# Sparse attention beside a mixture of experts: the weights of experts 10 to 15 loaded and split later, in halves, over the first 16 tiles

## The reference

```python
xn = _layernorm(x, axis=-1)
x = x + attn(xn, ...) + ffn(xn, ...)

# attn: 16 query heads, 4 key heads, two 32-wide parts (one with rope);
# keys and values of the first 896 tokens are averaged in 14 blocks of 64,
# the last 128 stay single
scores = (q_sem @ k_sem2 + q_geo @ k_geo2) * scale * exp(logit_scale)
probs = softmax(where(k_pos <= pos, scores, -1e9))
out = (probs @ v2) @ Wo

# ffn: 16 experts, the best 4 of each token
scores = softmax(x @ router_w.T + expert_bias)
top_w, top_idx = top_k(scores, 4); top_w = top_w / sum(top_w)
act = silu(x @ gate_proj[e]) * (x @ up_proj[e])      # 256 -> 224
out = sum over the 4 experts of top_w * (act @ down_proj[e])
```

## Time and profile before

| | us |
|---|---|
| median of 3 runs (lowest, highest) | 395.76 (393.83, 397.96) |
| profiled execution | 395.17 |
| its span | 393.4 |
| TensorE busy | 350.6 (89%) |
| VectorE busy | 242.4 (62%) |
| GpSimd busy | 232.0 (59%) |
| ScalarE busy | 182.6 (46%) |

### The profile page before, as it was taken

How to read it: one execution, slowest core, us unless ns; L and a number is a source line. 1 busy time by engine, 2 the same in 40 slices (tenths; PEclk the granted TensorE clock), 3 DMA queues, 4 the chain that set the end, 5 groups by cost and what they waited for, 6 DMA issues and landing times.

```text
span 393.4 us, 8217 instructions
## 1 busy us (share of the span) xinstructions
PE 350.6 (89%) x2085; PEld 287.6 (73%) x2086; DVE 242.4 (62%) x784; ACT 182.6 (46%) x530; POOL 232.0 (59%) x207
## 2 busy tenths in 40 slices
PE   0498997998979999987977999999999999999991
PEld 0393675645746677666876999999999999999881
DVE  3879996488458789852547455555555555555550
ACT  1540186458013344444455455555555555555550
POOL 0600456546664464659987466666666666666664
PEclk9998998699989999996998899999999999999996
DMA  7993112224146388863686476666776766666544
GB/s 247 361 314 89 55 60 84 75 80 125 69 147 209 114 257 257 248 213 86 174 176 100 71 113 107 112 107 107 110 113 108 111 112 112 109 108 107 70 52 53
DMA packets 50094, 52.33 MB, mean 133 GB/s; under 512 B 5632, under 2 KB 47120, under 8 KB 50072
## 3 DMA queue, kind: packets, MB, share of 16 engines
q0 software_dynamic: 14640, 19.34, 29.8%
q1 hardware_dynamic: 35432, 32.73, 29.1%
HBM read 30.14 MB, written 21.91 MB: 132 GB/s over the span
## 4 chain that ended last, share of the span: by engine, by line
PE 48%; DMA 18%; POOL 14%; issue 9%; DVE 6%; ACT 2%; POOLq 1%; SPq 1%; DVEq 0%; ACTq 0%
PE bank L1366 39%; DMA xn_by_expert<-x_all,slot_i 14%; POOL xn_by_expert L714 13%; PE bank L1728 4%; PE bank L1704 4%; DMA out_rows<-y,idx 2%; DMA x_all<-in_L_attn_x 1%; ACT x_all L763 1%; POOL wgu_lo L691 1%; DVE stats L954 1%; PE bank L1378 1%; DVE logit_left L1024 1%; DMA xg<-xn_by_expert 1%; POOLq L103 0%; ACT wgu_hi L815 0%
## 5 line engine op out<-in xcount | busy, mean ns | idle before, releaser
L741 POOL DMA_INDIRECT out_rows<-y,idx x79 | 124.5, 1576 | 66.3 <-ACT y L930 39.6
L714 POOL DMA_INDIRECT xn_by_expert<-x_all,slot_i x64 | 66.2, 1034 | 55.6 <-DMA xn_by_expert<-x_all,slot_i 33.7
L1366 PE MATMUL bank<-wgu_hi,xh 128*128 x158 | 65.9, 417 | 4.7 <-DVE wdn_lo L1195 2.6
L1346 DVE SCALAR_TENSOR_TENSOR act<-bank,xg,sg 128x224 f32<-128x224 f32 x79 | 35.6, 451 | 55.7 <-ACT sg L917 55.7
L1366 PE MATMUL bank<-wgu_lo,xh 128*128 x158 | 59.3, 375 | 0.0
L1366 PE MATMUL bank<-wgu_hi,xl 128*128 x158 | 58.8, 372 | 0.0
L917 ACT ACTIVATE sg<-bank 128x224 f32<-128x224 f32 x79 | 28.3, 358 | 62.3 <-PE bank L1366 62.3
L1338 DVE TENSOR_TENSOR xl<-bank,xh 128x256 fp32r<-128x256 f32 x79 | 33.5, 425 | 35.5 <-ACT xh L908 35.5
L1366 PE MATMUL bank<-wdn_hi,ah 112*128 x158 | 51.8, 328 | 0.6 <-issue 0.5
L1366 PE MATMUL bank<-wdn_hi,al 112*128 x158 | 44.8, 283 | 0.0
L1366 PE MATMUL bank<-wdn_lo,ah 112*128 x158 | 44.6, 282 | 0.0
(11 more groups left out here) (235 smaller groups left out, 658.2 us busy)
## 6 DMA issues: line engine op xcount, KB each, us to landing
xg<-xn_by_expert SPq DMA_DIRECT2D x79, 129.0 KB, 2.5
wgu<-in_L_ffn_gate_proj SPq DMA_DIRECT2D x16, 224.0 KB, 4.0
wgu<-in_L_ffn_up_proj SPq DMA_DIRECT2D x16, 224.0 KB, 4.6
wdn<-in_L_ffn_down_proj SPq DMA_DIRECT2D x16, 224.0 KB, 4.9
x_all<-in_L_attn_x SPq DMA_DIRECT2D x8, 256.0 KB, 5.0
xr<-in_L_attn_x SPq DMA_DIRECT2D x14, 128.0 KB, 2.2
out_rows<-xr SPq DMA_DIRECT2D x14, 128.0 KB, 3.8
out_rows<-y,idx POOLq DMA_INDIRECT x79, 3.8
```

Of the source, the lines that this page charges most:

```text
L714: gp.indirect_dma_start(xs_d, bass.IndirectOffsetOnAxis(slot_i[:, z, r:r + 1], 0), x_all[:, z, :], None).then_inc(xs_in[p], DMA)
L741: gp.indirect_dma_start(out_rows, bass.IndirectOffsetOnAxis(idx[r % RING][:, 0:1], 0), ysb[r % 4][:, :], None, compute_op=ALU.add).then_in ...
L1346: nc.vector.scalar_tensor_tensor(av[t.par][:, :], bank[2 + t.par][:, I:2 * I], xg[t.slot][:, D + 1:D + 2], sg[t.par][:, :], ALU.mult, ALU. ...
L1366: return nc.tensor.matmul(o, lhsT, rhs, start=start, stop=stop)
```

## The change

The experts' groups become (4, 5), (6, 7), (8, 9), (10, 11), (12, 13), (14, 15). SyncE loads (6, 7) after `store_sum(1)` and (8, 9) after `store_sum(3)`; (10, 11) behind tiles 0 to 3; (12, 13) and (14, 15) behind tiles 4 to 7. ScalarE splits (6, 7) in pair 3 as before, (8, 9) in pair 5, and the experts 10 to 15 in the steps 2 to 13 of the tile stage, one of the two copies per step. VectorE makes their low parts in the steps 4 to 15, one of the two differences per step. GpSimd's loop makes the low parts of 6 to 9 only. The written-out steps reach to 16 instead of 8, and TensorE waits for the tile's own expert up to tile 17. The planner gives every expert at least one task, so that the expert of task n is never above n.

```diff
-LATE = ((4, 5), (6, 7), (8, 9), (10, 11), (12,), (13,), (14, 15))
+LATE = ((4, 5), (6, 7), (8, 9), (10, 11), (12, 13), (14, 15))
...
-        SPLITS = ((), (4, 5), (), (6, 7), (8, 9), (10,), ())
-        HEAD = (11, 12)
+        SPLITS = ((), (4, 5), (), (6, 7), (), (8, 9), ())
         SENT = 11
         BETWEEN = (4, 5)
-        IN_LOOP = 13
+        IN_LOOP = 10
+        HIGH_FROM, LOW_FROM = 2, 4
...
         ROUND = 8
+        HEAD = 2 * ROUND
...
-            for r in range(-2, ROUND + 1):
+            for r in range(-2, HEAD + 1):
                 step(Tile(0, r))
             if carry:
-                carry()
-            with eng.Fori(1, rounds) as i:
+                carry(HEAD)
+            with eng.Fori(HEAD // ROUND, rounds) as i:
...
             load_residual(REMOTE - 1)
-            def load_behind(n, t):
-
-                for u in range(NB):
-                    sp.wait_ge(c_s[u], t)
-                load_late(n)
 
             for i in range(REMOTE - 3):
                 store_sum(i)
                 load_residual(i + 2)
-                if i < 3:
-                    load_late(i + 1)
-                else:
-                    load_behind(4, 2)
+                if i % 2:
+                    load_late(i // 2 + 1)
             store_sum(REMOTE - 3)
-            load_behind(5, 4)
...
             for j in range(RING // 2):
                 load_task(j, j)
+            load_late(3)
             for i in range(REMOTE - 2, REMOTE):
                 store_sum(i)
             for j in range(RING // 2, RING):
                 load_task(j, j)
-            load_late(6)
+            load_late(4)
+            load_late(5)
...
+            def split_high_part(e, part):
+                if part == 0:
+                    nc.scalar.copy(of_expert(wgu_h, e), of_expert(wgu, e))
+                else:
+                    nc.scalar.copy(of_expert(wdn_h, e), of_expert(wdn, e)).then_inc(w_hi, 1)
+
             def split_high(e):
-                nc.scalar.copy(of_expert(wgu_h, e), of_expert(wgu, e))
-                nc.scalar.copy(of_expert(wdn_h, e), of_expert(wdn, e)).then_inc(w_hi, 1)
+                for part in range(2):
+                    split_high_part(e, part)
...
-            def split_late(k):
-                if k == SENT:
...
-                split_high(k)
+            def split_late(k, parts=(0, 1)):
+                if 0 in parts:
+                    if k == SENT:
...
+                for part in parts:
+                    split_high_part(k, part)
...
                     for u in range(NB):
                         p_keep(u, Pair(0, REMOTE - 1))
-                    for k in HEAD:
-                        split_late(k)
...
-                if j.counts is None and j.r in (5, 6, 7):
-                    split_late(IN_LOOP + j.r - 5)
+                n = j.r - HIGH_FROM
+                if j.counts is None and 0 <= n < 2 * (E - IN_LOOP):
+                    split_late(IN_LOOP + n // 2, (n % 2,))
...
                 link(nc.vector.tensor_tensor(tasks[:, :], tiles_f[:, :], bound[:, 1, :], ALU.subtract))
+                link(nc.vector.tensor_scalar(tasks[:, :], tasks[:, :], 1.0, None, ALU.max))
...
-                if j.counts is None and j.r in (6, 7, 8):
-                    k = IN_LOOP + j.r - 6
-                    dve.wait_ge(w_lo, k)
-                    split_low(k)
+                n = j.r - LOW_FROM
+                if j.counts is None and 0 <= n < 2 * (E - IN_LOOP):
+                    k = IN_LOOP + n // 2
+                    if n % 2 == 0:
+                        dve.wait_ge(w_lo, k)
+                    split_low_part(k, n % 2)
...
-                    if t.counts is None and t.r <= ROUND + 1:
+                    if t.counts is None and t.r <= HEAD + 1:
                         pe.wait_ge(w_lo, pe.to_reg(e + 1))
```

More of the change, by code:

```diff
@@ L546, in steps @@
                 if carry:
-                    carry()
+                    carry(ROUND)
             for r in range(ROUND * rounds + 1, NS + 1):
@@ L873, in p_keep @@
                 last.then_inc(c_pT[u], 1)
-            def split_late(k):
-                if k == SENT:
[L877 to L881, removed]
-                split_high(k)
+            def split_late(k, parts=(0, 1)):
+                if 0 in parts:
+                    if k == SENT:
+                        for p in range(GT):
+                            act.wait_ge(xs_in[p], K * GROUPS * DMA)
+                    for n, ks in enumerate(LATE):
+                        if k == ks[0]:
+                            act.wait_ge(w_late[n], len(ks) * 3 * DMA)
+                for part in parts:
+                    split_high_part(k, part)
             def attention_act(t):
@@ L1190, in l_values, with split_low_part @@
                 nc.vector.tensor_copy(oT[u][:, 2 * g:2 * g + 2, :], bank[7][:, 0:2 * P].rearrange("p (j n) -> p j n", j=2)).then_inc(l_osb, 1)
+            def split_low_part(e, part):
+                if part == 0:
+                    dve.wait_ge(w_hi, e + 1)
+                    nc.vector.tensor_tensor(of_expert(wgu_l, e), of_expert(wgu, e), of_expert(wgu_h, e).bitcast(F32), ALU.subtract)
+                else:
+                    nc.vector.tensor_tensor(of_expert(wdn_l, e), of_expert(wdn, e), of_expert(wdn_h, e).bitcast(F32), ALU.subtract).then_inc(w_lo, 1)
             def split_low(e):
-                dve.wait_ge(w_hi, e + 1)
-                nc.vector.tensor_tensor(of_expert(wgu_l, e), of_expert(wgu, e), of_expert(wgu_h, e).bitcast(F32), ALU.subtract)
-                nc.vector.tensor_tensor(of_expert(wdn_l, e), of_expert(wdn, e), of_expert(wdn_h, e).bitcast(F32), ALU.subtract).then_inc(w_lo, 1)
+                for part in range(2):
+                    split_low_part(e, part)
             def keep_tables():
@@ L1679, in load_experts, with carry @@
                     known[first + k] = values[k]
-            def carry():
+            def carry(first):
                 for r in range(2):
-                    pe.reg_mov(carried[r], known[ROUND + r])
+                    pe.reg_mov(carried[r], known[first + r])
                 known.clear()
```

## The result

| | before | changed |
|---|---|---|
| median | 396.31 (4 runs) | 409.52 (4 runs, 409.29 to 410.07) |
| profiled execution | 395.17 | 409.47 |
| its span | 393.4 | 407.4 |

The changed kernel is slower: its time is 1.0408 of the one before, with an interval of 1.0356 to 1.046. The direction was forecast, the size was not: 9.1 us were forecast and 14.3 us came between the two profiled executions. On the median shown before, 395.76 us, the ratio stands for 411.9 us, above the upper end of the range (397.5 to 410).

The account below looks back on a forecast made before the run. The tile stage was taken to keep TensorE's pace, with only its start, gated by the dispatch, and run-up movable. 16.7 - 1.0 - 8.1 + 1.5 = +9.1 us on 395.17 made 404.3, given as 404.5 us; range 397.5 to 410.

Parts of the forecast that it names:

- Which views and which gate: Start of the tiles: the last scores, at 192.2, replace the dispatch, at 175.46, as the gate of tile 0.
- The loads in the attention: Pairs 3 and 5: late expert loads hold the splits and attends, with cold restarts; tile 0 16.7 us later (11.3 to 16.7).
- The entry: Ahead of tile 0: TensorE's idle shrinks from 3.19 to some 0.7 us and it may keep its clock; 1.0 us gained.
- The run-up: Early tiles: two TensorE gaps and their restarts go, 8.1 us gained; tile 8's load late behind weights, 1.5 us lost.
- the tile stage losing again what it gained: Sign of being wrong: the tile stage gives back its gain, pointing at tile 8's load or the scatters.
- the half splits: Twelve half splits on ScalarE (steps 2 to 13) and VectorE (4 to 15): costed at nothing, 0 to 2 us in all.
- the planner's instruction: Planner: one extra instruction on a 128x16 tile, 100 us ahead of any need; costed at nothing.
- the lighter dispatch: Dispatch: (10, 11), 12 and 13 no longer load beside it, but it is no gate any more; costed at nothing.
- The scatters beside VectorE's low parts: GpSimd's scatters in the tile stage: slowed by VectorE's differences beside them; taken as 0, bound 2.6 us.
- The hidden waits: Rival, faster: both groups land within ScalarE's cover, (6, 7) by 146.00, leaving only the gains; 386.3 us, chance 7%.
- The tile stage suffers too: Rival, slower: tile 8 late by 3 us and cold (+3.2), scatters held by VectorE (+2.6); 410.3 us, chance 15%.

Follow-up runs that it names:

- both repairs: Changed kernel with (6, 7) and (8, 9) loaded one turn earlier and tiles 8 to 11 loaded ahead of the last four experts: 384.19 us, ratio 0.9714.
- one group late in the kernel before: Kernel before with (6, 7) alone loaded one turn later, after the sum of pair 1, right ahead of (8, 9): 396.73 us, ratio 1.0029.
- tiles 4 and 5 first: Against the kernel with both repairs: tiles 4 and 5 loaded right behind tiles 0 to 3, ahead of (10, 11) and the last sums: 384.28 us.
- tiles first: Changed kernel with tiles 8 and 9 loaded ahead of (12, 13) and tiles 10 and 11 ahead of (14, 15): 401.92 us.
- empty issues: Changed kernel with (12, 13) and six 8 KB DMAs into scratch ahead of tile 8's load, (14, 15) after tile 11: 407.48 us.
- 8 idle products: Changed kernel with 8 products that nobody reads added in TensorE's gap before attend(4): 408.21 us.

## Why the prediction was right in its direction and wrong in its size

**Which views and which gate: right.** The loads of (6, 7) and (8, 9) hold ScalarE, ScalarE holds the attend, and the last scores replace the dispatch as the gate of tile 0. The experiments with the loads moved back show it for both groups together and for the second alone.

**The loads in the attention: 16.7 us forecast, 16.3 measured, and by luck, out of two wrong parts.** From VectorE's sum to the free split it took 151.15 - 139.50 = 11.7 and 176.29 - 165.03 = 11.3 us, not 13.17: the prediction took the place of (8, 9) as it stood, with (6, 7) in flight ahead of it. The time is saved before the loads, not in them: from the sum to the first issue it is 143.06 - 139.50 = 3.6 us instead of 146.33 - 141.03 = 5.3, from there to the free split 8.1 us instead of 7.9. The gaps were 6.3 and 5.8 us, where 8.2 and 7.7 had been forecast (the second with the 0.38 us of before). The first restart cost 158.33 - 152.82 = 5.5 instead of 151.37 - 147.83 = 3.5 us, 2.0 us and near the 1.7. The second cost 13.36 - 7.29 = 6.1 us: here the price from one row was far off. Gaps forecast 3.7 us too long and restarts 4.7 us too cheap nearly cancelled; and the changed kernel's execution came to pair 1's sum 1.5 us sooner. SyncE's store of the sum before is 1.5 us sooner too (130.13 against 131.66), ahead of the first load that the change moves, so I put this down to spread between executions.

**The entry: right.** 1.0 us forecast, 1.5 us measured. TensorE idled 1.01 us instead of 3.19 before tile 0 and stayed at the upper level (the last attend of the attention took 1.90 instead of 2.94 us). The gain reaches the tiles over SyncE: the last sums are stored sooner, and tile 4's load, which stands behind them, goes out 10.1 us behind tile 0's instead of 11.4.

**The run-up: here the prediction failed.** Its two gaps went as forecast (8.1 us by the rows, 8.6 us by the tiles' turns). The failed step is "late by as much as the 2.7 MB ahead of it take beyond their issue. I allow 0 to 3 us of wait and 0 to 1.7 us for a cold restart, and take 1.5 us lost". That term measured 7.8 us, with a wait of 6.0 us and the restart. The mechanism was named; its size was guessed and not worked out. The issue time in it was nearly right (11.0 us behind tile 4's load forecast, 11.8 measured). What was missing is the time of the bytes. With the 270 to 289 GB/s of the windows above, 2.75 MB take about 10 us; the twelve issues take 6.9 us (206.67 to 213.55). That alone would be some 3 us of wait. The rest fits the other traffic on the same engines: from the first of these issues to tile 8's landing (206.67 to 222.10) the window shows 262 GB/s, 4.0 MB, 1.3 MB more than the twelve loads; tiles 4 to 7 and the scatters were under way. Half the bytes with as many issues cut the wait to 0.79 us, and the other order removed it, with 5.8 us gained between tiles 4 and 14. With 7.8 for 1.5 the sum of the prediction is 15.4 us, against 14.3 us. The prediction's own sign of being wrong, "the tile stage losing again what it gained, which would point at tile 8's load", is what came.

**Costed at nothing, and rightly:** the half splits (from the turn of tile 9 to that of tile 14 the changed kernel keeps the pace of 2.38 us, 237.81 - 225.91 = 11.9 us; whole splits cost some 2.5 us), the planner's instruction, and the lighter dispatch, which was no gate. With both repairs it is the gate of tile 0 again, and there it counts.

**The scatters beside VectorE's low parts:** 0 was taken, and 0 it is. The 15 scatters from 207.44 to 248.72 took at most 1.62 us. In this order of work the difference ends as the scatter begins:

```profile
214.07 1.08 DVE L1198 TENSOR_TENSOR wgu_lo<-wgu,wgu_hi 128x896 fp32r<-128x896 f32 x1
```

It runs to 215.15, and the scatter beside it starts at 214.97 and takes 1.61 us. The row of 2.30 us in the kernel before was no stray, though. There VectorE makes both differences of an expert at once, and two more scatters begin inside one:

```profile
211.23 1.80 POOL L741 DMA_INDIRECT out_rows<-y,idx  x1 [0.34 <-issue]
213.66 2.10 POOL L741 DMA_INDIRECT out_rows<-y,idx  x1 [0.62 <-DMA out_rows<-y,idx]
```

```profile
213.24 1.08 DVE L1194 TENSOR_TENSOR wgu_lo<-wgu,wgu_hi 128x896 fp32r<-128x896 f32 x1
```

With 0.87, 0.66 and 0.39 us of the difference still to run these scatters took 2.30, 2.10 and 1.80 us; the one at 209.34, begun ahead of a difference, took 1.55. In the run with one group late in the kernel before, three begun with 0.66, 0.65 and 0.41 us left took 2.09, 2.67 and 2.45. So every scatter that began with 0.39 us or more of such a difference still to run took longer, in the kernel before by somewhat less than was left. This speaks against the inference of the Trainium skill (SBUF — State Buffer, "Who interferes with whom") that a `tensor_tensor` with both inputs in SBUF leaves the making of descriptors alone; no run was made for it, so another cause isn't ruled out. The halves cost nothing here by the moment at which the scatters begin, which the prediction did not foresee.

**The rivals.** The hidden waits did not come: the loads needed to be there by 146.00 and freed the split at 151.15. "The tile stage suffers too" came nearest by its number, 410.3 us, and was half right: tile 8 was late and cold, the scatters were not.

## What to carry to other kernels

A load that is moved one turn later in a queue is late by a whole turn where its user has no slack, and one turn of SyncE's list decided here between 409.5 and 390.8 us. When loads are put behind others in a queue, count the bytes ahead of the next urgent one at the rate that the windows show, not only the issues, and with them what other queues move meanwhile. And look for the second gate right behind the first: it can make a delay nearly free (the kernel before, tiles 6.5 us late and no slower that the runs can tell), and it can eat most of a repair (tiles 4 and 5 first).

## What was not expected of the hardware

The price of a gap on TensorE is no constant. The gap of 6.34 us was followed by some 4 us at the lower level and cost 2.0 us; one of 5.83 us, in the same kernel, was followed by 12 us of unbroken work at 0.50 to 0.54 and cost 6.1 us. It isn't the same in every execution either: behind gaps of 6.74 us (tiles first) and 6.59 us (empty issues) in the same place, pair 6 took 11.1 and 11.2 us instead of 13.4, a cost of 3.8 and 3.9 us. A gap of 2.77 us there (8 idle products) was enough for the same 4.67 us attend. The same work without a gap ran at 1.00. Why the lower level lasts so much longer in pair 6 than in pair 4 stays open.
